# Biased attention with three banks for its head projections, an own bank for the turned rows and its norms placed earlier; causal attention with wide probability sums

## The reference, cut to what matters

```python
# causal self attention, 16 heads of 8
q, k, v = split_heads(x @ Wq + bq), split_heads(x @ Wk + bk), split_heads(x @ Wv + bv)
att = softmax(where(tril, q @ k.T * hd**-0.5, -inf))
y = (att @ v) @ Wo + bo

# cross attention with a position bias, 16 heads of 64
q = inputs_q @ Wq; k = inputs_kv @ Wk; v = inputs_kv @ Wv
a = q @ k.T / sqrt(64) + rel_bias[bucket]
a = where(mask, a, lowest)
out = (softmax(a) @ v) @ Wo

# top-1 expert: its router's logits for the normed result of the part before
logits = x @ router_w.T + router_b
```

## Time and profile before

| | |
|---|---|
| time, median of 3 runs | 1814.85 us (1810.28 to 1815.51) |
| profiled execution, its time | 1815.88 us |
| its span in the trace | 1814.1 us |
| TensorE busy | 1703.9 us (94%) |
| VectorE busy | 1202.5 us (66%) |
| ScalarE busy | 894.9 us (49%) |
| GpSimd busy | 629.4 us (35%) |
| TensorE clock granted, mean | 0.987 |
| causal stage, from its first scores to the biased stage's first | 1216.9 to 1383.8 us |
| biased stage, to its last projection | 1383.8 to 1743 us |

### The profile page before, as it was taken

The page is one execution under the profiler, slowest core; times in us unless marked ns, Lnnn a source line. Parts: engine busy times, 40 slices in busy tenths (PEclk is TensorE's granted clock), DMA queues, the critical chain, the costliest instruction groups (busy, mean ns, idle before and its releaser), DMA issues. The chain is left out here.

```text
span 1814.1 us, 48107 instructions
## 1 busy us (share of the span) xinstructions
PE 1703.9 (94%) x18760; PEld 1267.9 (70%) x18760; DVE 1202.5 (66%) x2924; ACT 894.9 (49%) x1930; POOL 629.4 (35%) x760
## 2 busy tenths in 40 slices
PE   7999999998999999999799999988998999999878
PEld 5566666666888888888556667766766877777643
DVE  6677777655778787776453222238987777777757
ACT  1444444446666666676332213337874555444434
POOL 2111111112334344443214633343432444444537
PEclk9999999999999999999999999999999999999989
DMA  9300000002444444444320002311011333333311
GB/s 330 96 1 0 0 0 0 0 1 75 142 141 147 141 147 142 139 149 141 122 82 30 30 23 78 120 51 31 29 38 32 101 96 105 97 100 96 108 34 41
DMA packets 176162, 146.77 MB, mean 81 GB/s; under 512 B 12168, under 2 KB 154299, under 8 KB 175506
## 3 DMA queue, kind: packets, MB, share of 16 engines
q1 hardware_dynamic: 172690, 139.12, 24.0%
q0 software_dynamic: 3328, 5.58, 0.9%
HBM read 79.00 MB, written 67.43 MB: 81 GB/s over the span
## 5 line engine op out<-in xcount | busy, mean ns | idle before, releaser
L1061 ACT ACTIVATE xa_probs<-ps,xa_top 128x128 f32<-128x128 f32 x512 | 146.4, 368 | 146.1 <-DVE xa_top L1164 145.5
L1105 POOL TENSOR_TENSOR xa_probs<-xa_probs,xa_total 128x512 f32<-128x512 f32 x128 | 133.3, 1041 | 200.8 <-DVE xa_total L1159 200.8
L154 POOL TENSOR_TENSOR rstd<-var_eps,minus_half 128x2 f32<-128x2 f32 (+1 forms) x116 | 92.1, 794 | 302.0 <-DVE var_eps L148 301.7
L977 PE MATMUL ps<-xa_probsT,xa_kv 128*128 128x512 f32 x256 | 134.1, 605 | 15.5 <-DMA xa_probsT<-turned_blocks 14.3
L1164 DVE TENSOR_REDUCE xa_top<-ps 128x4 f32<-128x512 f32 x128 | 88.3, 690 | 87.0 <-PE ps L968 86.0
L956 PEld LDWEIGHTS ps<-xa_kvT,pack_latent 128*128 128x128 f32 x512 | 97.8, 192 | 65.6 <-issue 57.4
L987 PEld LDWEIGHTS ps<-pack_latent,xa_attnT 128*128 128x128 f32 x1024 | 133.8, 192 | 12.2 <-issue 6.4
L968 PE MATMUL ps<-xa_kvT,xa_qT 128*128 128x128 f32 x1024 | 135.4, 275 | 1.4 <-ACT xa_probs L1061 1.4
L987 PE MATMUL ps<-pack_latent,xa_attnT 128*128 128x128 f32 x1024 | 134.4, 275 | 0.3 <-DVE X L1141 0.3
L956 PE MATMUL ps<-xa_kvT,pack_latent 128*128 128x256 f32 x512 | 132.2, 384 | 1.4 <-PEq L343 1.4
L395 PEld LDWEIGHTS ps<-pack_moe,la_hid 128*128 128x128 f32 x1024 | 121.0, 192 | 17.4 <-issue 15.3
(11 more groups left out here) (347 smaller groups left out, 3740.0 us busy)
## 6 DMA issues: line engine op xcount, KB each, us to landing
turned_blocks<-xa_blocks SPq DMA_DIRECT2D x128, 256.0 KB, 3.2
xa_probsT<-turned_blocks SPq DMA_DIRECT2D x128, 256.0 KB, 3.0
turned_blocks<-ba_blocks SPq DMA_DIRECT2D x64, 256.0 KB, 2.5
ba_probsT<-turned_blocks SPq DMA_DIRECT2D x128, 128.0 KB, 2.7
expert_weights<-experts_dram SPq DMA_DIRECT2D x8, 768.0 KB
result_pairs<-zeros SPq DMA_DIRECT2D x1, 4096.0 KB, 29.9
ca_got<-result_pairs SPq DMA_DIRECT2D x16, 256.0 KB, 2.7
slot_rows<-zeros SPq DMA_DIRECT2D x1, 2880.0 KB, 18.7
```

The source lines that it names most:

```text
L154: pool.tensor_tensor(m.rstd[:, 0:tiles], m.var_eps[:, 0:tiles], m.minus_half[:, 0:tiles], ALU.pow).then_inc(sem.rstd, 1)
L977: pe.matmul(bank(ATTN_BANK + u % 2), kv[:, k, seq, :], probsT[:, u % SETS].rearrange("p g n q -> p n g q"), start=True, stop=True)\
L1061: exp = act.activation(probs[:, s % 4, n], bank(s % 2)[:, KEYS * n:KEYS * n + KEYS], ACT.Exp, bias=top[:, s % 4, n:n + 1], scale=-1.0)
L1105: pool.tensor_tensor(probs[:, u % 4], probs[:, u % 4], over(total[:, u % 4], 2, KEYS), ALU.mult).then_inc(probs_ready, 1)
```

## The change

In the causal stage the sums of the probabilities leave `attend`. A new function `sum_rows` makes them once a step, behind the numerators of both units, with moving operands of 256 columns (all four sequences) in place of 64: 8 matmuls for a step in place of 32. `attn_done` is raised once a step.

In the biased stage,
- head projection n goes to bank 6, 2 or 7 (n modulo 3) and waits for the copy of n-3; the semaphores of the copies are split so that DVE's two copies have their own (`proj_dve`);
- the turned rows and the router's logits move from the upper half of bank 5 to bank 7 (`TOP_BANK`); `turn_top` waits for the copy of head projection 5, head projection 2 for the router's logits of an earlier step;
- PE's wait for `topT_ready` moves from ahead of `project(s-1, 1)` to behind it;
- ACT's copy 9 and its copy of the turned rows (`top_rows`) move ahead of `exp(s, 2)`, and copy 10 ahead of `exp(s, 3)`;
- DVE's `normed` of tiles 2 and 3 and of tiles 0 and 1 move ahead of `bias_and_top(s, 2)`.

```diff
@@ causal_attention, TensorE
-                        for part in range(2):
-                            at = NS * part + SEQ * seq
-                            for par in range(2):
-                                for j in range(J):
-                                    lhsT = w["head_ones"][:, par, :] if part else vheads[:, k, par, seq, j, :]
-                                    mm = pe.matmul(bank(ATTN_BANK)[FJ * j:FJ * j + FJ, at:at + SEQ], lhsT,
-                                                   probsT[:, u, b, j, SEQ * par:SEQ * par + SEQ],
-                                                   start=(par == 0), stop=(par == 1))
+                        for par in range(2):
+                            for j in range(J):
+                                pe.matmul(bank(ATTN_BANK)[FJ * j:FJ * j + FJ, SEQ * seq:SEQ * seq + SEQ],
+                                          vheads[:, k, par, seq, j, :], probsT[:, u, b, j, SEQ * par:SEQ * par + SEQ],
+                                          start=(par == 0), stop=(par == 1))
+
+                def sum_rows():
+
+                    by_seq = probsT[:].rearrange("p u b j n -> p (u b) j n")
+                    for par in range(2):
+                        for j in range(J):
+                            mm = pe.matmul(bank(ATTN_BANK)[FJ * j:FJ * j + FJ, NS:], w["head_ones"][:, par, :],
+                                           by_seq[:, :, j, SEQ * par:SEQ * par + SEQ], start=(par == 0), stop=(par == 1))
                     mm.then_inc(attn_done, 1)
@@
                         attend(later(step, -1), 1 - k, 0)
                         attend(later(step, -1), 1 - k, 1)
+                        sum_rows()
@@ causal_attention, VectorE
-                    dve.wait_ge(attn_done, count(step, UNITS, UNITS))
+                    dve.wait_ge(attn_done, count(step, 1, 1))
@@ biased_attention
-        ATTN_BANK, OUT_BANK = 3, 5
+        ATTN_BANK, OUT_BANK, TOP_BANK = 3, 5, 7
@@
         def proj_bank(n):
+            if n < HEADS_PROJ:
+                return bank((b.proj_banks + (TOP_BANK,))[n % 3])
             return bank(b.proj_banks[n % 2])
@@ TensorE
                     if n == 0:
                         pe.wait_ge(in_ready, count(step, 1, 1))
-                    copied(pe, step, n - 2)
+                    if n == 1:
+                        copied(pe, step, -1)
+                    if n == 2:
+                        reach(pe, top_logits_ready, count(step, 1, -LAG - 1))
+                    if n >= 3:
+                        copied(pe, step, n - 3)
@@
-                    if exists(top):
-                        pe.wait_ge(topT_ready, count(top, 1, 1))
                     if before:
                         project(last, 1)
                     if exists(top):
+                        pe.wait_ge(topT_ready, count(top, 1, 1))
                         top_logits(top)
@@ ScalarE
                         copy(coming, 1 - k, 8)
+                        copy(coming, 1 - k, 9)
+                    if exists(top):
+                        top_rows(top)
                     if here:
                         exp(step, 2)
                     if ahead >= 1:
-                        copy(coming, 1 - k, 9)
+                        copy(coming, 1 - k, 10)
                     if here:
                         exp(step, 3)
-                    if exists(top):
-                        top_rows(top)
                     if ahead >= 1:
-                        copy(coming, 1 - k, 10)
                         copy(coming, 1 - k, 11)
@@ VectorE
                         turn(step, 0)
                         turn(step, 1)
+                    normed(later(step, 2), (2, 3))
+                    if ahead >= 2:
+                        normed(later(step, 2), (0, 1))
+                    if here:
                         bias_and_top(step, 2)
                         bias_and_top(step, 3)
-                    normed(later(step, 2), (2, 3))
                     if ahead < 0:
                         route.less_top(dve, 0)
                         route.choose(dve, 0)
                     if here:
                         summed(step, 2)
                         summed(step, 3)
-                    if ahead >= 2:
-                        normed(later(step, 2), (0, 1))
```

More of the change, by code:

```diff
@@ L1747, in biased_buffers @@
     b.proj_odd = sem("proj_odd")
+    b.proj_dve = sem("proj_dve")
     b.proj_banks = (6, 2)
@@ L2118, in copy_turned @@
                     if b == 0:
-                        reach(act, attn_done, count(step, UNITS, u - 1))
+                        reach(act, attn_done, count(step, 1, 0))
                     act.wait_ge(probs_turned, count(step, 2 * UNITS, 2 * u + b + 1))
@@ L2251, in copy_next_q @@
                     dve.wait_ge(biased.proj_done, n + 1)
-                    dve.tensor_copy(next_q(n), next_q_bank(n)).then_inc(biased.proj_odd, 1 if n < 2 else 5)
+                    dve.tensor_copy(next_q(n), next_q_bank(n)).then_inc(biased.proj_odd, 1 if n < 2 else 3)
                 def scale_mask():
@@ L2360, in biased_attention @@
     MOVES = 2 * 16
-    COPIES = PROJ // 2
+    EVEN_COPIES, ODD_COPIES, DVE_COPIES = 6, 4, 2
     NORMS = 4
@@ L2412, in copied @@
         def copied(engine, step, n):
-            reach(engine, (proj_even, proj_odd)[n % 2], count(step, COPIES, n // 2 + 1))
+            if n in (3, 7) and is_first(step):
+                reach(engine, proj_odd, ODD_COPIES)
+            elif n in (3, 7):
+                reach(engine, proj_dve, count(step, DVE_COPIES, n // 4 + 1 - DVE_COPIES))
+            elif n % 2:
+                reach(engine, proj_odd, count(step, ODD_COPIES, (-1, 1, 5, 9, 11).index(n)))
+            else:
+                reach(engine, proj_even, count(step, EVEN_COPIES, n // 2 + 1))
         def projected(k, n):
@@ L2540, in turn_top @@
                     pe.wait_ge(ln.normed, count(top, NORMS, NORMS * (LAG + 3) - 2) - 2 * without_inputs)
-                    reach(pe, top_logits_ready, count(top, 1, 0))
+                    if top[0] + top[1] + LAG + 1 < STEPS:
+                        copied(pe, later(top, LAG + 1), 5)
+                    else:
+                        reach(pe, top_logits_ready, count(top, 1, 0))
                     for t in range(2):
-                        mm = pe.transpose(bank(OUT_BANK)[:, NS + P * t:NS + P * t + P], xn[:, 2 + t, :], w["ident"][:])
+                        mm = pe.transpose(bank(TOP_BANK)[:, P * t:P * t + P], xn[:, 2 + t, :], w["ident"][:])
                     mm.then_inc(top_turned, 1)
@@ L2547, in top_logits @@
                     for t in range(2):
-                        mm = pe.matmul(bank(OUT_BANK)[:, NS + E1 * t:NS + E1 * t + E1],
+                        mm = pe.matmul(bank(TOP_BANK)[:, E1 * t:E1 * t + E1],
                                        topT[:, t, :], w["router1"][:], start=True, stop=True)
@@ L2612, in top_rows @@
                     reach(act, topT_kept, count(top, 1, 0))
-                    act.activation(topT[:], tiles_of(bank(OUT_BANK)[:, NS:]), ACT.Copy).then_inc(topT_ready, 1)
+                    act.activation(topT[:], tiles_of(bank(TOP_BANK)[:, 0:NS]), ACT.Copy).then_inc(topT_ready, 1)
                 def body(step, k, ahead):
@@ L2742, in top_scores @@
                     dve.tensor_tensor(m.top_logits[:, bass.ds(count(top, 2, 0), 2), :],
-                                      bank(OUT_BANK)[:, NS:NS + 2 * E1].rearrange("p (t e) -> p t e", e=E1),
+                                      bank(TOP_BANK)[:, 0:2 * E1].rearrange("p (t e) -> p t e", e=E1),
                                       over(w["router_b"][:], 1, 2), ALU.add).then_inc(top_logits_ready, 1)
@@ L2747, in copy @@
                     dve.wait_ge(proj_done, count(step, PROJ, n + 1))
-                    dve.tensor_copy(projected(k, n), proj_bank(n)).then_inc(proj_odd, 1)
+                    dve.tensor_copy(projected(k, n), proj_bank(n)).then_inc(proj_dve, 1)
                 def turn(step, u):
```

2 lines of the change are left out of this document (1 added, 1 removed).

## The result

| | before | changed |
|---|---|---|
| time, median | 1812.57 us (4 runs, 1808.62 to 1815.51) | 1789.26 us (4 runs, 1786.89 to 1795.65) |
| ratio | | 0.9869, 95% interval 0.9848 to 0.9891 |
| profiled execution, span | 1815.88, 1814.1 us | 1789.93, 1788.1 us |
| ahead of the first causal scores | 1216.9 us | 1212.8 us |
| causal stage | 166.9 us | 164.9 us |

What follows compares the result with a forecast made beforehand. PE was taken to set the biased stage's pace, so its waits count. From the profiled 1815.9 us, -25.4 for the biased stage and -1 for the causal gave 1789.5; forecast band 1784 to 1797, range 1781 to 1803.

Steps and rivals of the forecast that it cites:

- biased stage: 13 steps x (1.38 + 0.55 - 0.26), plus 1.8 at steps 0 and 1 and 1.9 at the end: -25.4 us, bounds -16 and -32.
- Norms first: Biased stage: four norms take 1.1 us in DVE's 1.19 us idle, beside idle POOL; PE gains 1.38 us a step.
- Three banks: Biased head projections: eight at the pace of one that doesn't wait, 0.55 us a step; bounds 0 and 0.6.
- The loads: Biased stage, attend waiting for probsT loads: some half of the steps wait, costing about 0.3 us a step; period 19.9.
- Steps 0 and 1: Start of biased stage: turn_inputs waits go, but attend(0, 0) already waits for loads; 1.8 us gained.
- what follows step 14's first scores: End of biased stage: norms cost DVE 0.6 in step 15, but project no longer waits for copied rows; 1.9 us gained.
- The clock: Biased stage window: the clock was read as full at 0.97, with no term for it.
- The causal part: Causal stage: wide sums cost 0.2 x 14 = +3 us, 4 us of instruction waits go; -1, between -6 and +5.
- Norms not hidden: Rival, biased stage: norms take 2.8 us in the new place; 1795, or 1805 if all comes through. Chance 0.10.
- Banks or instructions: Rival, biased stage: heads keep 7.5 us, or the denser list brings more short issue waits; 1798. Chance 0.12.
- It does not do what it says: Rival: turn_top is released no earlier, or the stall moves whole to the loads; 1811 to 1816. Chance 0.05.
- Loads as the loop: Slower rival, biased stage: the way from second transpose to landing takes 12.05 us, period 22.1; 1825. Chance 0.05.

Runs made afterwards that it cites:

- the loads aside: Changed kernel with the loads of units 0 and 1 landing in unused memory, so attend waits for none after the first step: 1786.43 us, ratio 0.9830.
- edit of the queue: Changed kernel with SyncE storing both units of a pair before waiting for the first, then loading both: 1777.07 us, ratio 0.9774.

## Why the prediction was right, and where its terms were off

The forecast was 1789.5 us; the median is 1789.3 and the profiled run 1789.9. The total is better than its parts:

| part | forecast | profiled runs | by itself |
|---|---|---|---|
| biased stage | -25.4 | -20.7 | ratio 0.9879 (some -22) |
| causal stage | -1 | -2.0 | ratio 0.9977 (some -4) |
| ahead of both | 0 | -4.2 | |
| behind both | 0 | +0.9 | |

**Ahead of the stage.** 4.2 us of the total stand where not one line differs. Over the fourteen traces the causal stage starts at anything from 1212.8 to 1221.1 us, and the kernel before varied from 1810.1 to 1823.0 within one series. Some of it is in waits for loads of a part in front. This row is of the changed kernel, and the same row of before had 14.3 us in 14:

```profile
PE ps L977 <- DMA xa_probsT<-turned_blocks: 12.3, 13, 1.8
```

The prediction had no term for it, and nothing in the change accounts for it, so I take it for luck. That it is chance from one execution to the next isn't shown: the same program again started at 1214.3, nearer to 1212.8 than to the 1216.9 of before, of which there is one trace. It covered for the biased stage's short term.

**Norms first: right.** 1.08 us for four, forecast 1.1, beside an idle POOL; the earlier trace rows has 2.82 for the same four. Where they stay late they keep the long price (1.32 and 1.29 us for two in the run with late norms, beside POOL instructions of 1.07 and 2.12 us). The rule of the Trainium skill, "SBUF — State Buffer" (who interferes with whom), that the port pair of DVE and GpSimd is held by one of them at a time, agrees in both places, and the rival built on 2.8 us fell. DVE's last transpose ends 0.88 us behind the next scores; forecast 0.9.

**What the prediction didn't say of them:** by itself the move is worth nothing. The prediction gave all 1.38 us to the norms. It had PE's wait for the turned rows at `top_logits` already, but gave that move no share, and took ACT's order as the reason why the rows would be there. The runs show that with PE's list of before the wait of `project(s-1, 1)` for the turned rows comes at once, and that with PE's new list it is gone, with ACT in either order. It is a gain of two edits together, and ACT's part of the change is idle.

**Three banks: 0.40 in place of 0.55 us a step** (7.54 - 6.96, the prediction's own figures, is even 0.58). The step that failed is "eight projections at the pace of one that doesn't wait: 8 x 0.87". The heads take 7.13, not 6.96: 64 pairs of 0.109 us, 0.05 more at the first pair and 0.10 more at the last, ahead of `project`. The window of head projection 1 in the earlier trace rows showed the pace alone and not the two ends.

**The loads: 0.7 in place of 0.26 us a step.** This is the term that was most off. The working had both numbers and put them together wrongly: a loop of 20.0 us through the loads and a list of 19.66 on PE can't give a mean period of 19.9. The loop is a floor under every step, and its own spread comes on top. With the loads aside PE's list is 19.74. From the last transpose to `attend` PE alone needs 9.51 us, as seen in steps without a wait. In steps 3 to 14 of the changed kernel it took between 9.51 and 11.07, 9.99 on average: in ten of the twelve it was longer than 9.52. A wait costs its own length and some 0.2 us of restart (0.95 of wait in the step shown, 10.66 - 9.51 = 1.15 of time), and no later part of a step gives it back. The prediction's 9.93 was that of one step of before; in the changed kernel the last load lands 9.70 us behind the transpose on average, and an `attend` that waited starts 0.25 behind that, together 9.95. One more wait, of 1.59 us, stands at the start of the stretch over which 20.43 is taken. So 12 steps from 2 to 14 brought 16.0 us, where the forecast had 20.0. Even of the 16.0 some 1.4 are no effect of the lists: in two of these steps of before, with periods of 22.38 and 22.33 us, the heads took 8.25 and 8.29 us in place of 7.55, with one pause of 0.6 us in each at full clock, and the changed kernel's trace has no such step in that stretch. Steps 0 and 1 brought 1.85 (forecast 1.8), and what follows step 14's first scores 2.9 (forecast 1.9, and 1.67 for one more step).

**The clock: put at nothing.** The prediction called 0.97 full. Over 361 us it means, as an estimate, some 21 us at 1.2 GHz; in the changed kernel's window of 340 us it is 0.96, some 27 us. From the first scores of step 14 on PE is busy 43.6 us in place of 41.6 for the same matmuls, at 0.79 in place of 0.85. So some 2 us of what the end saved in waits went to the clock.

**The causal part: within its bounds, by two terms that were each larger.** The step grew by 0.27 us, from 8.91 to 9.18 (forecast 0.2, bounds 0 and 0.4), for the reason given: what stands behind the second `attend` went from 1.03 to 1.45 us (forecast 1.4). In the trace of after it shows as 15 waits for ACT's copy. Idle time for "issue" fell by 5.6 us, not 4 (6.5 of the 8.2 was in L2010). +3.8 and -5.6 make -1.8; the stage shows -2.0. But that is one trace of each: over all of them the stage is no shorter with the wide sums (165.1 us on average in the four with the old sums, 165.8 in the eight with the wide ones). That these waits are instruction supply is argued and not shown. For it speaks that they are fewer in every trace with 48 instructions less a step, 2.6 to 4.9 us against 5.3 to 8.3. Nothing here shows what PE waited for in them.

**The rivals.** Norms not hidden: fell. Banks or instructions: fell, though 0.15 of its 0.55 us was true. It does not do what it says: fell for the change as a whole, but its case, a stall that moves whole to the next wait, is what the norms alone show. Loads as the loop: the mechanism is there, in most steps, at 20.4 us. It is slower than before only from 21.6, and the mean never came near. The edit of the queue shows that it was the next bound, and that what made it one was unit 1's wait of 3.8 us in the queue.

## What to carry to other kernels

When a stall goes, write out the next loop with every step of it and take its mean, not its best case: the period is at least the larger of the engine's list and that loop, never something between. In this case moving work earlier paid only once the next wait behind it was off too, so look up every wait between it and the end of the step; here the norms alone gave nothing, all the rest without them nothing, both together 1.2%. Read the granted clock of each stretch beside its waits: a stretch full of waits can also run slower when it does run. A queue that waits for a store to land before it issues the next store is the place to look at as soon as loads end last.

## What the runs showed of the hardware

- A round trip of one unit through DRAM: from a store's issue to the load's issue that waits for it, 2.2 to 2.4 us in the step shown, and from that to the landing 4.2 us, in other steps 3.2. The Trainium skill, "DMA: Bandwidth & Descriptors" (Anatomy of one DMA — SWDGE (gpsimd) path), gives some 2.0 us as the fixed cost, whatever the size, of a transfer that goes out by GpSimd's path. These go out by SyncE's queue, for which that section has no figure; the store's 2.2 to 2.4 us, its 256 KB included, lie near it. With two stores in flight, issued at 1508.83 and 1509.42, the first landed at 1511.05 and the second at 1511.99: they overlap.
- The same four norms cost DVE 1.08 us beside an idle POOL and 2.82 beside a busy one; each late pair ends 0.09 us behind the POOL instruction that it overlaps. Moving them shortened DVE's busy time in the stage by 20.5 us.
- A run of matmuls that waits for nothing keeps its pace from kernel to kernel in most steps (7.21 us for the heads' 128 in the changed kernel, in that with the loads aside and in that with two stores), and has single pauses of 0.2 to 0.7 us without a releaser in a few. At the clock of 1.2 GHz a pair of these matmuls takes 0.21 us in place of 0.109. The rest is not so steady: over the fourteen traces all that runs ahead of the causal stage, with waits for DMAs in it, moves by up to 8 us. A difference of less than some 5 us in this kernel is read in its stage, and not in the total alone.
- "issue" waits also stand in code that no edit touches, and move: 1.8 us once at L1976 in the changed kernel, 4.0 us once at the same line in that with two stores.
